# First experts' chunks in the last routing of a decoder layer: products moved one step earlier, both first down products side by side, weight loads behind the routing

## The reference, cut to what matters

```
x = layernorm(x + self_attention(x))
x = layernorm(x + cross_attention(x, ctx))              # x2 below
scores = softmax(x @ gate.T, axis=-1).transpose(0, 2, 1)  # a sequence: 16 experts x 256 tokens
topk_w, topk_idx = top_k(scores, 32)                      # "the routing"
x_tok = take(x, topk_idx)                                 # gathered rows
h = gelu(x_tok @ Wg[e].T) * (x_tok @ Wu[e].T)             # 512 hidden columns per expert
eo = (h @ Wd[e].T) * topk_w                               # "the down product"
out = zeros.at[topk_idx].add(eo) + shared_expert(x)       # scatter-add to the tokens
x = layernorm(x + out)
```

## Time and profile before

| what | value |
|---|---|
| median of three runs | 3184.5 us |
| the profiled execution's own time | 3182.56 us |
| its span, first to last instruction | 3180.7 us |
| mean granted TensorE clock | 0.991 |
| share of the span in which PE is busy | 97% |
| share in which DVE, ACT, POOL are busy | 71%, 67%, 50% |
| last routing, from the last output products to `col_done` | about 2297 to 2344 us |

### The profile page before, as it was taken

One profiled execution on the slowest core, in us unless ns is written; L12 is line 12 of the kernel. 1 busy time (PEld: TensorE's weight loads), 2 busy tenths in 40 slices (PEclk: granted clock), 3 DMA queues, 4 the chain that ended last, 5 costly groups with the idle time before them and its releaser, 6 DMA issues. The chain is left out here.

```text
span 3180.7 us, 78651 instructions
## 1 busy us (share of the span) xinstructions
PE 3088.8 (97%) x22624; PEld 2899.9 (91%) x22624; DVE 2257.4 (71%) x6562; ACT 2145.7 (67%) x6926; POOL 1596.1 (50%) x2912
## 2 busy tenths in 40 slices
PE   6999999999999998999999999999879999999998
PEld 5999999999999987999999999999868888889998
DVE  5777777787777877778878777787745455544565
ACT  6878888888887877787877777777734444442222
POOL 3666766766676765333333333333446666663000
PEclk8999999999999999999999999999989999999999
DMA  6444444444434440111111211111235444533333
GB/s 181 117 120 124 127 125 121 120 120 125 123 111 116 128 133 24 54 57 46 62 45 48 64 45 48 61 45 47 96 113 119 100 97 100 125 60 82 122 125 106
DMA packets 193684, 300.70 MB, mean 95 GB/s; under 512 B 33856, under 2 KB 134080, under 8 KB 192704
## 3 DMA queue, kind: packets, MB, share of 16 engines
q1 hardware_dynamic: 168768, 262.91, 27.9%
q0 software_dynamic: 24576, 33.57, 6.2%
HBM read 116.02 MB, written 67.11 MB: 58 GB/s over the span
## 5 line engine op out<-in xcount | busy, mean ns | idle before, releaser
L962 POOL TENSOR_SCALAR ca_prob<-ca_prob,ca_inverse 128x120 f32<-128x120 f32 x1024 | 357.0, 370 | 635.5 <-DVE ca_inverse L1264 633.9
L665 ACT ACTIVATE sa_prob<-sa_prob,sa_shift 128x128 f32<-128x128 f32 (+1 forms) x1024 | 453.5, 461 | 2.6 <-DVE sa_shift L718 2.6
L1210 ACT ACTIVATE ca_prob<-bank,ca_shift 128x120 f32<-128x120 f32 x1024 | 354.7, 367 | 11.5 <-DVE ca_shift L1258 9.3
L460 POOL TENSOR_SCALAR sa_prob<-sa_prob,sa_inverse 128x128 f32<-128x128 f32 x512 | 200.9, 392 | 230.9 <-DVE sa_inverse L726 217.0
L718 DVE CUSTOM_DVE_ANT_0 sa_prob<-bank,sa_mask 128x128 f32<-128x128 f32 (+1 forms) x1024 | 304.7, 352 | 6.8 <-PE bank L138 2.9
L136 PE MATMUL bank<-sa_ow,sa_y_hi 128*128 128x256 f32 x1024 | 279.6, 304 | 0.0
L136 PE MATMUL bank<-sa_kvT_a,sa_q 128*128 128x128 f32 (+1 forms) x1024 | 251.4, 281 | 17.8 <-DMA sa_q<-sa_q_tile 17.0
L138 PE MATMUL bank<-sa_kvT_b,sa_q 112*128 112x128 f32 (+1 forms) x1024 | 261.6, 281 | 0.0
L749 DVE TENSOR_TENSOR sa_pT_lo<-bank,sa_pT_hi 128x384 fp32r<-128x384 f32 x512 | 258.3, 544 | 1.8 <-ACT sa_pT_hi L650 1.8
L138 PE MATMUL bank<-sa_ow,sa_y_lo 112*128 112x256 f32 x1024 | 258.8, 283 | 0.0
L462 POOL TENSOR_SCALAR sa_prob<-sa_prob,sa_inverse 128x256 f32<-128x256 f32 x512 | 248.1, 485 | 0.0
(11 more groups left out here) (258 smaller groups left out, 12022.3 us busy)
## 6 DMA issues: line engine op xcount, KB each, us to landing
sa_q<-sa_q_tile SPq DMA_DIRECT2D x128, 288.0 KB
sa_q<-sa_q_tile SPq DMA_DIRECT2D x160, 112.0 KB
mid_x2T<-ca_x2T SPq DMA_DIRECT2D x32, 512.0 KB, 3.0
ex_sx<-mid_x2T SPq DMA_DIRECT2D x32, 512.0 KB, 3.3
sa_q<-sa_q_tile SPq DMA_DIRECT2D x304, 32.0 KB, 2.9
sa_xT_raw<-in_xT SPq DMA_DIRECT2D x32, 256.0 KB, 2.8
sa_q<-sa_q_tile SPq DMA_DIRECT2D x32, 256.0 KB
sa_x_res<-in_x SPq DMA_DIRECT2D x32, 256.0 KB, 2.8
```

The lines of the kernel that those rows point to most:

```text
L460: pool.tensor_scalar(prob[:, r, hh, 0:P], prob[:, r, hh, 0:P], inverse[:, r, 2 * hh:2 * hh + 1], 1.0, ALU.mult, ALU.mult)
L665: act.activation(prob[:, r, hh, cols], prob[:, r, hh, cols], ACT.Exp, bias=shift[:, r, n:n + 1], scale=-1.0, accum_out=total[:, r, n:n + 1 ...
L962: ins = pool.tensor_scalar(prob[:, r, t, hh], prob[:, r, t, hh], inverse[:, r, n:n + 1], 1.0, ALU.mult, ALU.mult)
L1210: act.activation(prob[:, r, t, hh], SC[g % 2][:, n * S:n * S + S], ACT.Exp, bias=shift[:, r, n:n + 1], accum_out=total[:, r, n:n + 1]).the ...
```

## The change

The part that held three things is split in two: part LAST = 4 holds only the last `h_hi` and `h_lo` of a chunk, part ROWS = 5 the rows and the down product. The table is rewritten, the banks change their roles, both first down products stand in one place, and the loads move.

```
-EXPERTS_AT = {10: ((0, FT),), 11: ((1, 0),), 12: ((1, 1),), 13: ((1, 2),), 14: ((1, 3),), 15: ((1, FT),),
-              23: ((2, 0),), 29: ((2, 1),), 30: ((2, 2),), 31: ((2, 3),)}
+LAST, ROWS = FT, FT + 1
+EXPERTS_AT = {8: ((0, ROWS),), 9: ((1, 0),), 11: ((1, 1),), 12: ((1, 2),), 13: ((1, ROWS),), 14: ((1, 3),), 22: ((1, LAST), (2, 0)),
+              23: ((2, 1),), 29: ((2, 2),), 30: ((2, 3),), 31: ((2, LAST),)}
...
-    DB, GB, UB, XT = bank[0:2], bank[2:4], bank[4:6], bank[6:8]
+    DB, XT, GB, UB = bank[0:2], bank[2:4], bank[4:6], bank[6:8]
...
+    def downs(J, m):
+
+        if isinstance(J, int) and J == 0 and m in (DL, DL + 1):
+            return (0, 1) if m == DL else ()
+        return (m - DL,)
...
                         sp.wait_ge(first.lo_done, (e + 1) * (N_W // 512))
+                        sp.wait_ge(first.col_done, BODIES)
...
-                if isinstance(J, int) and J == 0 and n == 2:
+                if isinstance(J, int) and J == 1 and n == 2:
                     sp.wait_ge(first.o_mm, B * NP)
                     for (raw, _, _), name in zip(ahead.shared, ("sg", "su", "sd")):
...
+                if isinstance(J, int) and J == 0 and n == 0 and f == 1:
+                    pe.wait_ge(first.o_read, B)
                 wg, wu = [(weights(w_hi, e, part, F), weights(w_lo, e, part, F)) for part in (WG, WU)]
...
-            if f == FT:
+            if f == ROWS:
                 for work in (down, rows) if down_first(J, m) else (rows, down):
                     work(J, m)
...
-                if isinstance(J, int) and J == 0 and n == 0:
-                    pe.wait_ge(first.o_read, B)
                 need(pe, x_in[i], J * (8 * XBODY * TILES) + 16 * TILES * (n // 2 + 1))
...
         def down(J, m):
-            n = m - DL
-            if exists(J, n):
...
+            for n in downs(J, m):
+                if exists(J, n):
...
-                if f > 0:
+                if 0 < f <= FT:
...
-                if isinstance(J, int) and J == 0 and m == 3:
+                if isinstance(J, int) and J == 1 and m == 3:
                     act.wait_ge(ahead.shared_in, 48)
```

More of the change, by code:

```diff
@@ L1399, in ex_body @@
         for m in range(XBODY):
-            for part in range(FT + 1):
+            for part in range(ROWS + 1):
                 ex_part(J, m, part)
@@ L1603, in part @@
         def part(J, n, f):
-            if f < FT:
+            if f != ROWS:
                 return
@@ L1702, in down @@
         def down(J, m):
-            n = m - DL
-            if exists(J, n):
[L1705 to L1719, removed]
+            for n in downs(J, m):
+                if exists(J, n):
+                    i, (e, _) = n % 2, of_chunk(J, n)
+                    if isinstance(J, int) and J == 0 and n == 0:
+                        pe.wait_ge(first.col_done, BODIES)
+                    split_done(J, n, 1)
+                    need(pe, hlo_done, n_of(J, n, FT))
+                    need(pe, act_out, n_of(J, n - 1))
+                    need(pe, dve_out, n_of(J, n - 1))
+                    wd = weights(w_hi, e, WD, C), weights(w_lo, e, WD, C)
+                    for t in range(CHUNK // P):
+                        ts = slice(t * P, t * P + P)
+                        to = DB[t // 2][:, (t % 2) * C:(t % 2) * C + C]
+                        for f in range(FT):
+                            mm = three(pe, to, h_hi[:, i, f, ts], h_lo[:, i, f, ts], wd[0][:, f], wd[1][:, f], f == 0, f == FT - 1)
+                        if t % 2:
+                            mm.then_inc(d_mm.own, 1)
         def shared_body(J):
@@ L1810, in down @@
         def down(J, m):
[L1811 to L1820, removed]
+            for n in downs(J, m):
+                if exists(J, n):
+                    i, (_, c) = n % 2, of_chunk(J, n)
+                    need(act, added[i], added_by(J, n - 2))
+                    need_alone(act, d_mm, n_of(J, n, 2, -1), spare_act)
+                    for t in range(2):
+                        j = c * TILES + t
+                        ins = act.activation(out[:, i, t], DB[0][:, t * C:t * C + C], ACT.Copy,
+                                             scale=weight_of[:, expert_at(J, n), j:j + 1])
+                    ins.then_inc(act_out, 1)
         def shared_body(J):
@@ L1890, in down @@
         def down(J, m):
-            n = m - DL
-            if exists(J, n):
-                i, (_, c) = n % 2, of_chunk(J, n)
-                need(dve, added[i], added_by(J, n - 2))
-                need_alone(dve, d_mm, n_of(J, n, 2), spare_dve)
-                for t in range(2, TILES):
-                    j = c * TILES + t
-                    ins = dve.tensor_scalar(out[:, i, t], DB[1][:, (t - 2) * C:(t - 1) * C], weight_of[:, expert_at(J, n), j:j + 1],
-                                            None, ALU.mult)
-                ins.then_inc(dve_out, 1)
+            for n in downs(J, m):
+                if exists(J, n):
+                    i, (_, c) = n % 2, of_chunk(J, n)
+                    need(dve, added[i], added_by(J, n - 2))
+                    need_alone(dve, d_mm, n_of(J, n, 2), spare_dve)
+                    for t in range(2, TILES):
+                        j = c * TILES + t
+                        ins = dve.tensor_scalar(out[:, i, t], DB[1][:, (t - 2) * C:(t - 1) * C], weight_of[:, expert_at(J, n), j:j + 1],
+                                                None, ALU.mult)
+                    ins.then_inc(dve_out, 1)
         def shared_body(J):
```

4 lines of the change are left out of this document (2 added, 2 removed).

## The result

The changed kernel takes 3190.68 us in the median of 15 runs (3188.76 to 3193.76), the kernel before 3183.84 (3180.89 to 3186.33): a ratio of 1.0022, 95% interval 1.0015 to 1.0028. The forecast was 3188, the range 3180 to 3193. The medians lie 6.8 us apart, just past the 6.4 us (0.2%) that were to count as none; the interval reaches down to 0.15%, so on which side of that mark the difference lies isn't settled. The profiled execution took 3190.66 us, its span 3188.9.

A forecast was written before the change was run, and what follows sets the result against it. TensorE, busy 97% of the span, bounds the kernel; only its idle or low-clock time can move. Terms 7.0 - 2.9 + 0 + 0.5 = +4.6 us gave 3189.1 on the 3184.5 median, stated as 3188, range 3180 to 3193.

The forecast's parts named there:

- part one: Last routing up to the scores' transposes: residual behind chunk 0's first `hid`, `h_lo` held by GpSimd's split; 7.0 us late.
- part two: From the scores' transposes to the columns and first down product: 18.1 us instead of 21.0, so 2.9 won.
- part three: Both down products, from the columns to chunk 3's first product: 33.3 to 35.6 us against 34.4, taken as no change.
- chunk 3's products: TensorE's products of chunk 3 may run cold: 0 to 2.2 us, taken as 0.5.
- the shared split: Shared weights' split, moved one body on under cover of transposes and down product: 0, bounds 0 and +0.6 us.
- Rival A: `h_lo` not held, or for one instruction only; chunk 1's gathers then decide, columns +0.2 us: 3184, chance 0.19.
- The stall: VectorE's 3.66 us stand before an `h_lo`, read as an instruction fetch stuck behind the weight loads; goes when they move.
- the new wait: Second down product waits for the banks that VectorE still copies out: 1.1 us.
- chunk 2's products: TensorE's products of chunk 2, behind both down products: 11.23 to 13.47 us.
- the bare rows of chunk 3: Rows of chunk 3, no longer covered by a down product: 3.64 us + 0.4 for `h_hi` and `h_lo`.
- Part four: Moved loads start with the columns, hidden, delaying chunk 2's gathers under cover; split and bank roles cost nothing: 0.
- Rival B: Moved loads hold GpSimd's first gather until they end: +4.5 us on top of 4.6, 3192.5, chance 0.18.

The follow-up runs named there:

- e1: Changed kernel with the table's front half (chunk 0's rows and quarters, chunk 1's rows) as in the kernel before: 3187.3 us, ratio 1.0005.
- e2: Changed kernel with only chunk 0's first quarter moved, behind slot 11 with the second instead of behind slot 9: 3187.59 us, ratio 1.0014.
- e3: Changed kernel with GpSimd waiting for its own last instruction before each of six pieces of expert 1's weight split: 3194.94 us, ratio 1.0031.
- e8: Changed kernel with the loads spread: expert 2's behind chunk 2's rows, expert 3's and the shared expert's behind chunk 3's: 3192.77 us, ratio 1.0019.
- e4: Changed kernel with the loads and the shared weights' split back in their old place, without the wait for the columns: 3195.79 us, ratio 1.0035.
- e9: e1 with the loads spread as in e8: 3186.86 us, ratio 1.0002.
- e6: Kernel before the change with the same edit as e3, a wait before each piece of GpSimd's second split: 3186.43 us, ratio 1.0004.
- e15: e16 with both down products together again as in the change, and chunk 3's gathers held behind the second: 3183.04 us, ratio 0.9991.
- e16: e11 with chunk 1's down product back behind chunk 3's rows, and chunk 3's gathers held until the first down product is read out: 3176.92 us, ratio 0.9974.
- e11: Changed kernel with the old front order except chunk 0's rows early, gaps as in e3, and loads spread as in e8: 3190.02 us, ratio 1.0013.
- e13: e3 with chunk 3's four gathers held until VectorE has read out chunk 1's down product: 3189.45 us, ratio 1.0014.

## Why the prediction was right

It was right in sum and in mechanism, with terms that missed in both directions. Against the +4.6 us forecast the profiles give +6.2: part one 1.9 more, part two 0.5 less, part three 1.4 less, chunk 3's products 1.1 more, the shared split 0.6 more. That these cancel to 1.6 is luck, and so is that the kernel before came 0.7 us below the median the forecast started from. The prediction gave 0.70 to no difference beyond 0.2% and 0.23 to slower; the medians fall into the second by 0.4 us.

**Part one, +7.0: measured +8.9.** Each link stood: `hid` ahead of the residual, `ca_var_eps` at 0.17 us instead of 2.80 because GpSimd was idle, GpSimd's chain 8 us late, the `h_lo` held to its end. e1 undid the order and the delay went; e2 undid a part and 4.75 of it went; e3 took the hold away. Two sizes were off, both in the same direction. The first `hid` came 5.53 us behind its first product, not 4.35 (1.2 us), and VectorE stood 1.03 us ahead of the scores, which no term had. Rival A is out: the hold was of the whole chain, and without it (e3) chunk 1's rows put the scores 6.4 late, not at +3.

The Trainium skill (SBUF — State Buffer, "Who interferes with whom") says that whoever issues first has the shared ports "for the whole instruction". One instruction of the chain is 1.26 us; the hold lasted to the end of the chain, over nearly all six (7.54, 7.50 in e8, 7.48 in e4) or over what was left of them where `h_lo` came later (4.56 in e2, 3.02 before, 2.72 in e1, 1.47 in e9). In all seven profiles without gaps `h_lo` ended 0.55 or 0.56 us behind the chain. With 0.18 us between them the same `h_lo` took 1.38, as the Trainium skill's rule has it: it ended 0.57 us behind the one GpSimd instruction that it had met. So the rule holds for instructions with a gap, and back to back the measurement goes beyond it.

**Part two, -2.9: measured -3.4** (17.57 us from the transposes to the first down product, 18.1 forecast). The stall goes with the loads, as read, though e4, which has them back, shows 1.9 us and not 3.7: see e6. That it is an instruction fetch is not shown. The Trainium skill (Runtime: NRT & Kernel Launch, "Instruction fetch mechanics") says of the cost of crossing from one fetched block of instructions to the next that it is "mostly hidden". The profiles list packets of instructions in two queues and don't say whose they are; one of them lies inside the stall of the kernel before (2323.1 to 2326.8), and none can be told to be VectorE's.

**Part three, 0 (bounds -1.0 and +1.2): measured -1.4** in the changed kernel. The terms were near: the new wait 1.18 (1.1), chunk 2's products 11.22 (11.23 to 13.47), the bare rows of chunk 3 3.95 (4.04). It came out at the good end because chunk 2 ran at the upper clock (granted 1.00); then chunk 3 ran at a granted clock of 0.87, +1.6 where 0.5 was taken. But the comparison was with a profile of before whose chunk 2 took 2.2 us longer, at 0.82. e15 against e16 is the price without these stalls: +4.4. So part three's zero was right for this pair of kernels and wrong as a price of the down products' place. What the forecast didn't see is that the old order was held up by GpSimd's late first gather (3.4 us behind the columns, 0.8 in e16), and that it would be the better one without that.

**Part four, 0: right.** e8 moved the loads again and nothing changed. Rival B named a danger at the right place with the wrong cause: GpSimd's first gather came 3.2 us behind the columns, no later than before, and engines do come late behind the down product, but with the gathers, not with the loads. In the changed kernel none was caught. The shared split cost 0.64, at the bound of 0.6; e4 shows what it would have cost unmoved, 3.4.

Two slips in the working change little: the prediction counts five waits of TensorE and names six (they do sum to 21 us), and 4.69 MB at 361 GB/s take 13.0 us, not 12.5.

What stays open: why VectorE and ScalarE are caught behind a run of eight gathers in e1 to e4, e6 and e8 to e11 and not in the kernels before and after, whose eight gathers run just as long; and what decides whether chunk 2's products are granted the upper clock (11.2 us in after, e2, e8, e13 and e15, 12.7 to 14.0 in the others).

## What to carry to other kernels

Before expert work is put ahead of a step of a serial chain, follow what that step releases on other engines: here one `hid` of 0.7 us ahead of the residual made it wait for TensorE's products, and moved GpSimd's weight split onto VectorE's critical part. A long GpSimd run, of elementwise pieces or of gathers, can hold VectorE or ScalarE, so look at what they do beside it. Breaking the split alone gained nothing in either kernel (e3, e6); it paid only with the gathers' run shortened as well (e15, e16). An order that looks bad (a down product apart from its twin) may only be held up by something else; remove that first, then compare the orders.

## What was not expected of the hardware

- Back-to-back GpSimd instructions kept a VectorE instruction with two SBUF inputs out for as long as they lasted: 7.48 to 7.54 us of six, 4.56 to 1.47 where it came later, each time to 0.55 us behind the last of them; 1.38 with gaps of 0.18 us.
- Beside GpSimd's runs of eight gathers an instruction of VectorE or ScalarE started only 1.75 to 1.96 us behind the last gather (seven cases; 1.14 and 0.36 in two more, and in e6 one late start fell inside the run), though neither takes part in them. In the three kernels with four gathers in a row none was held there.
- With a load burst of 4.7 MB at one place of the program VectorE stalled for 3.7 us (before, e6; 0.7 in five kernels without it), and at another the burst made no difference (after against e8).
- TensorE's granted clock differed between profiles of nearly the same order: the same 48 products of chunk 2 took 11.2 us at 1.00 or up to 14.0 at 0.78 (e9), and in e1, e3 and e4 this makes up a good part of the loss behind the down product.
